# A scan kernel whose TensorE units are placed in halves and thirds between the steps of the scan

## The reference, cut to what matters

```python
# layers 0 and 1, each: router, shared experts, 8 routed experts
s = sigmoid(concat([xf, tf]) @ router_W); gates = top2(s + bias), normalised
y = (silu(xf @ w1) * (xf @ w3) @ w2 + sum_e gates_e * (gelu(xf @ W1e) @ W2e)) / scale
# layer 2
def step(h, z_t):
    gate = sigmoid(h @ Wh.T + z_t @ Wz.T + b)
    h_new = tanh(h * leak + gate * z_t)
    return h_new, h_new
# layer 3
q, k, v = split(x @ c_attn_w + c_attn_b)
out = softmax(causal(q @ k.T / sqrt(8))) @ v @ c_proj_w + c_proj_b
```

## Time and profile before

| | us |
|---|---|
| median of 3 runs | 444.67 |
| lowest and highest run | 443.91, 444.80 |
| the profiled execution's own time | 444.19 |
| its span (first to last instruction) | 442.4 |
| from the start to the first STEP | 44.6 |
| from the first STEP to the last | 294.4 |
| from the last STEP to the end | 103.4 |
| PE busy in the span | 416.9 |
| DVE busy | 292.5 |
| ACT busy | 249.1 |
| POOL busy | 85.5 |

### The profile page before, as it was taken

How to read it: one execution, slowest core, us unless ns; L and a number is a source line. 1 busy time by engine, 2 the same in 40 slices (tenths; PEclk the granted TensorE clock), 3 DMA queues, 4 the chain that set the end, 5 groups by cost and what they waited for, 6 DMA issues and landing times.

```text
span 442.4 us, 13043 instructions
## 1 busy us (share of the span) xinstructions
PE 416.9 (94%) x4550; PEld 307.7 (70%) x4550; DVE 292.5 (66%) x983; ACT 249.1 (56%) x869; POOL 85.5 (19%) x366
## 2 busy tenths in 40 slices
PE   2999999899999999999999999899999999999994
PEld 1788778668777677777766666656766677777772
DVE  5786566765765675565665766538664999985662
ACT  3551745644644654573575536756567647556882
POOL 7320311321321231141232121211121000000000
PEclk9999999999999999999999999999999999999998
DMA  8510000000000000000000000000000100100001
GB/s 304 191 18 7 6 1 1 1 1 1 1 2 1 1 2 1 2 1 1 1 0 1 4 1 3 0 2 2 2 2 4 26 2 4 27 4 4 15 17 25
DMA packets 11222, 7.70 MB, mean 17 GB/s; under 512 B 8983, under 2 KB 10263, under 8 KB 11159
## 3 DMA queue, kind: packets, MB, share of 16 engines
q1 hardware_dynamic: 10727, 6.61, 4.8%
q10 hardware_dynamic: 432, 0.27, 0.3%
HBM read 5.39 MB, written 1.05 MB: 15 GB/s over the span
## 4 chain that ended last, share of the span: by engine, by line
PE 68%; ACT 12%; DVE 6%; issue 3%; POOL 0%; DVEq 0%; ACTq 0%
PE ybk L1066 15%; PE cbk L1234 12%; PE ybk L1190 6%; PE hid L1214 4%; DVE cbk L1560 4%; ACT dd L987 3%; ACT hb L913 3%; PE hid L1166 2%; ACT hs L992 2%; PE hid L1116 2%; PE hid L1091 2%; PE vbk L1214 2%; PE cbk L1238 1%; PE cbk L1166 1%; PE hid L1171 1%
## 5 line engine op out<-in xcount | busy, mean ns | idle before, releaser
L1234 PEld LDWEIGHTS cbk<-hs,rec 128*128 128x128 f32 x512 | 76.3, 188 | 65.6 <-ACT hs L992 60.9
L1560 DVE TENSOR_TENSOR_SCAN cbk<-dd 128x24 f32<-128x24 f32 x256 | 55.8, 218 | 95.9 <-ACT dd L987 92.4
L1234 PE MATMUL cbk<-hs,rec 128*128 128x8 f32 x512 | 93.7, 255 | 8.2 <-ACT hs L992 2.7
L803 POOL TENSOR_TENSOR dd<-hs,leak 128x8 f32<-128x8 f32 x256 | 55.4, 216 | 228.4 <-ACT hs L992 225.6
L1066 PE MATMUL ybk<-hg,down 128*128 128x256 f32 x352 | 95.9, 397 | 0.6 <-DVE hg L1439 0.6
L992 ACT ACTIVATE hs<-cbk 128x8 f32<-128x8 f32 x256 | 45.3, 177 | 66.7 <-DVE cbk L1560 66.0
L987 ACT ACTIVATE dd<-cbk 128x8 f32<-128x8 f32 x256 | 46.3, 181 | 56.9 <-PE cbk L1234 56.0
L1214 PE MATMUL hid<-xsp,up 128*128 128x256 f16 x510 | 70.5, 277 | 0.3 <-DVE lg L1378 0.3
L1066 PEld LDWEIGHTS ybk<-hg,down 128*128 128x128 f32 x352 | 60.5, 191 | 6.0 <-DVE hg L1439 1.1
L1214 PEld LDWEIGHTS hid<-xsp,up 128*128 128x128 f16 x510 | 49.9, 108 | 6.7 <-issue 0.9
L1439 DVE TENSOR_TENSOR hg<-hb,hid 128x512 f32<-128x512 f32 x50 | 33.7, 676 | 3.0 <-PE hid L1052 2.7
(11 more groups left out here) (240 smaller groups left out, 647.0 us busy)
## 6 DMA issues: line engine op xcount, KB each, us to landing
qz<-up_in SPq DMA_DIRECT2D x3, 512.0 KB, 7.2
out_dram<-silu SPq DMA_DIRECT2D x4, 256.0 KB, 2.9
x<-x_in SPq DMA_DIRECT2D x7, 128.0 KB, 8.9
down<-down_in SPq DMA_DIRECT2D x1, 768.0 KB, 9.4
att<-att_in SPq DMA_DIRECT2D x1, 743.0 KB, 10.0
down<-down_in SPq DMA_DIRECT2D x1, 640.0 KB, 6.1
kp<-mrow SPq DMA_DIRECT2D x32, 4.0 KB
qz<-rows SPq DMA_DIRECT2D x32, 2.0 KB, 1.8
```

The lines of the kernel that those rows point to most:

```text
L803: tts(dd[:, t % ZR, 1, :, 2], hs[:, t, :], leak[:, 0:1].broadcast_to([P, B]), ALU.mult).then_inc(decay, 1)
L1234: pe.matmul(cbk[c % 2][:, o:o + B], wh, hs[:, t, :], start=False, stop=True, skip_group_check=True).then_inc(gate_pre, 1)
L1560: nc.vector.tensor_tensor_scan(vps[chunk_of(t) % 2], dd[:, t % ZR, 0].rearrange("p b o -> p (b o)"), dd[:, t % ZR, 1].rearrange("p b o -> ...
```

## The change

E, SA and SB become three parts for the planner, each of two matmuls, .218, .218 and .219 us instead of .655 in one piece. Y becomes as many parts as it has matmuls (two), .435 us each. K and Q become two parts of .215. C becomes .435 and .22. The parts of one unit keep their order, other units or a STEP may come between them, and the bank stays taken from the first part until it is emptied. The waits stand in front of part 0 only, and the signal behind the last part. The number of matmuls in the units is the same.

The second edit is `PATIENT` = .12: until the first STEP is planned, the planner may take a unit that starts up to .12 us later than the first possible one, if it stands earlier in `plan`. Before, this was .03 everywhere.

The core of the diff:

```diff
-EAGER = .03
+EAGER, PATIENT = .03, .12
+THIRDS = (.218, .218, .219)
...
-        return {"pe": (.0017 * n * min(512 // n, SHARED[key[2]] if key[3] == "s" else E),)}
+        return {"pe": (.0017 * n,) * min(512 // n, SHARED[key[2]] if key[3] == "s" else E)}
...
-        "GT": {"pe": (.13,), "act": (.27,)}, "SA": {"pe": (.655,), "act": (.5,), "dve": (.61,)},
-        "SB": {"pe": (.655,), "dve": (.61,)}, "E": {"pe": (.655,), "act": (.5,)}, "M": {"pe": (.22,), "dve": (.6,)},
+        "GT": {"pe": (.13,), "act": (.27,)}, "SA": {"pe": THIRDS, "act": (.5,), "dve": (.61,)},
+        "SB": {"pe": THIRDS, "dve": (.61,)}, "E": {"pe": THIRDS, "act": (.5,)}, "M": {"pe": (.22,), "dve": (.6,)},
...
-        "K": {"pe": (.43,), "act": (.49,)}, "Q": {"pe": (.43,), "act": (.49,)}, "QZ": {"dve": (.27, .27)},
+        "K": {"pe": (.215, .215), "act": (.49,)}, "Q": {"pe": (.215, .215), "act": (.49,)}, "QZ": {"dve": (.27, .27)},
...
-        at, _, _, family = min((f for f in found if f[1] == eng and f[0] <= t0 + EAGER), key=lambda f: f[2:3] + f[:1])
+        patience = EAGER if (("STEP", 0), "pe") in end else PATIENT
+        at, _, _, family = min((f for f in found if f[1] == eng and f[0] <= t0 + patience), key=lambda f: f[2:3] + f[:1])
...
-        if eng == "pe":
+        if eng == "pe" and not part:
             if key in banked:
...
-                m.then_inc(pe_done, 1)
+                if last:
+                    m.then_inc(pe_done, 1)
...
-            def times_x(into, c, l, name, i):
+            def times_x(into, c, l, name, i, third):
...
+                n = CHUNKS[c] * B
+                for of in (2 * third, 2 * third + 1):
+                    i2, j = divmod(of, 3)
+                    a = UP[name, l][0] + (i + i2) * P
+                    pw, px = ((0, 0), (0, 1), (1, 0))[j]
+                    m = pe.matmul(into[:, i2 * n:i2 * n + n], up[:, pw, a:a + P], x_part(c, l, px, slice(0, n)), start=j == 0,
+                                  stop=j == 2)
```

72 lines of the change are left out of this document (35 added, 37 removed).

## The result

The changed kernel takes 439.95 us (median of 4 runs, 439.82 to 440.5). The kernel before, run beside it, takes 444.74 (4 runs, 443.91 to 445.52). The ratio is 0.9898, with a 95% interval from 0.9879 to 0.9917: faster by 1%, 4.8 us. The prediction was 441.0 us, with a range from 438.6 to 443.8.

A forecast was written before the change was run, and what follows sets the result against it. PE was taken to bound prologue and tail, while PE work that finds room in a 1.12 us slot costs nothing. Prologue -1.9, slots +1.0 and tail -2.6 sum to -3.5 us: 441.0 us, range 438.6 to 443.8.

The forecast's parts named there:

- Prologue: Up to the first STEP: less foreign work ahead, partly replaced by waits for DVE; -1.9 us, between -2.6 and -.9.
- Slots: The 255 slots of the recurrence: fuller slots gain nothing, which ones are long changes; +1.0 us, between 0 and +2.5.
- V: Slots: V of tile 2 moves from the tail into a slot, which then lasts 1.58 us; +.46.
- MT: Slots: four pairs of MT become three and two single ones; -.25, if a single one costs .15.
- the overfull ones: Slots holding as much as Y and GT, .13 us too long each: seven against two before; +.7.
- Tail: Behind the last STEP: PE loses 4.0 us of units, DVE 2.1; -2.6 us, between -1.5 and -4.0.
- nearer to DVE's share: Tail: of PE's 4.0 us and DVE's 2.1 us removed, the gain was put at -2.6 us.
- Sum: Whole kernel: -1.9 + 1.0 - 2.6 = -3.5 us, giving 441.0 us.
- Rival 1: DVE bounds the tail and the prologue waits more for it; about 443.0 us; chance .16.
- Rival 2: Slots: split units hold banks across STEPs, so STEPs wait and slots last .13 longer; 446 us; chance .11.
- Rival 3: Tail: work left behind step 255 doesn't set the end, tile 3's chain does; 444 us; chance .10.
- Rival 4: Better: full 4.0 in the tail, -2.4 in the prologue, nothing lost in slots; 438.3 us; chance .07.

The follow-up runs named there:

- pe_extra: The kernel before, with the product matmuls of all 32 A units of tile 2 issued twice (64 matmuls more): 450.91 us, ratio 1.0141.
- dve_extra: The kernel before, with the maximum of eight A units of tile 2 repeated on DVE into an array nobody reads: 447.28 us, ratio 1.0057.
- thirds_whole: The changed kernel with E, SA and SB in one piece again, the rest of the change kept: 441.83 us, ratio .9960 to the kernel before.
- no_patience: The changed kernel with PATIENT back at .03, all splits kept: 444.43 us, ratio 1.0014 to the kernel before.

## Why the prediction was right, step by step

- **Prologue**: -1.9 forecast, -1.64 measured, and the first STEP at 42.98 is inside the 42.5 to 43.0 named. The mechanism was right: less foreign work, and in its place waits of PE for DVE ahead of Y of chunk 0. The replay had three of about .2 us there, the trace has two of .41. M is still 676 ns. That the number came within .3 us is partly luck, since the first STEP of one prologue spreads by .6 to .8 us from profile to profile. What the prediction didn't separate: patience alone gives -2.6 (42.05), and the splits take .9 of it back. "A third of an E as cover" was counted as help, and in sum the finer units were no help.
- **Slots**: +1.0 forecast, +1.21 measured, 295.60 in the 295 to 296 named, and the median slot is 1.12 us as before. Slot by slot against 1.12 us: V +.46 as forecast, a third slot of 1.58 (1.59). MT was mis-sized: -.25 forecast, 0 measured, because a single MT costs .26 (1.38 us) and not .15. The table load's slot went from 2.34 to 2.46, +.12, where I had 0. All other slots together +.65, where I had +.8 (the overfull ones and the denser work). Of the 36 slots with eight product matmuls 32 last 1.12 us, so their price held.
- **Tail**: -2.6 forecast, -4.17 measured, and the last STEP to the end took 99.22 us where 100.5 to 101 were named. This is the mis-sized term, and -4.17 is just outside its own bounds of -1.5 to -4.0. It lies in the body: -4.16 in the profile, -3.7 as the mean over the kernels with one list (91.63 against 95.33). The list of removed units was right, with 4.0 us of PE. DVE's 2.1 was too much: six QZ of .343 count their overlap, has 9.2 us for 32 of them, .29 each, and so 1.7. The step that failed was "nearer to DVE's share". The body got shorter by 3.7 to 4.2 us, which is all of PE's 4.0 and over twice DVE's 1.7. It had been argued with DVE at 92% of a stretch shorter by 4.0 us, so that PE would wait for the maxima; measured, DVE stood at 58.08 of 66 us and PE's time without work fell from 2.0 to 1.3 us. pe_extra measured that added work of PE counts in full, and dve_extra that DVE's counts at .7 to .8. But thirds_whole and no_patience won only 1.3 and 4.2 us for 3.0 and 6.1 us off PE, so the full share isn't a rule either, and why it came out full in this list stays open.
- **Sum**: -3.5 forecast, -4.6 measured in the span. The tail's term is 1.6 us off, and the prologue's and the slots' are .3 and .2 off the other way. So the time, 439.95, is 1.05 below the forecast, closer than its largest term by luck. The worst sum of the bounds, -.9 + 2.5 - 1.5, is +.1 or 444.3 to 444.6 us, so the range left out .5 to .8 of it, not .3.
- **Rival 1** (DVE bounds the tail; 443.0) falls as a whole, with 99.22 us of tail, where it wanted over 101.5, and DVE at 58.08 of 66, 88%, where it wanted over 92. Its mechanism has a part, by dve_extra and thirds_whole.
- **Rival 2** (banks held across STEPs; 446) falls: that needs 35 more slots .13 too long, or +4.5 us, and all slots together became 1.2 us longer. (Its 45 slots would be 5.9 us and 446.9, not 446.)
- **Rival 3** (what is left behind step 255 doesn't set the end; 444) falls: with work moved out the end came earlier in every kernel, and with work put in for tile 2 (pe_extra) later, by all of it.
- **Rival 4** (full 4.0 in the tail; 438.3) was right on the tail, and neither on the prologue (-2.4) nor on the slots (nothing lost).
- Not in the prediction: that the moments at which the clock rises and falls can move. It took the half clock at 12 to 13 us for granted in both kernels. Between before and after the fall changed nothing at the end (8.04 and 8.03 us), and the rise came .9 us earlier, which may hold a few tenths of the 1.64. In other versions of the kernel the fall decided a us or more.
